# A graph layer: v projected inside the score stage and the skip term inside the aggregation, from stored parts

## The chip, the cores and the metric

The kernel runs on one core of a Trainium2 chip. The metric is the device time of one execution in microseconds (us), the median of several runs. Besides the runs there is one profiled execution, whose trace gives every time shown below. PE is the matmul engine, DVE, ACT and POOL are VectorE, ScalarE and GpSimd, SP is the engine that only issues transfers and waits. A q behind an engine's name (SPq, ACTq) marks what its sequencer does.

## What is computed

A graph layer on 2,500 nodes with 512 channels and 40,000 edges, then a global mixing block and a gated feed-forward block. The change touches only the graph layer's two attention rounds:

```
for l in range(2):
    q = (x @ Wq[l] + bq[l]).reshape(N, H, D)      # N 2500, H 8 heads, D 64
    k = (x @ Wk[l] + bk[l]).reshape(N, H, D)
    v = (x @ Wv[l] + bv[l]).reshape(N, H, D)
    a = (q[dst] * k[src]).sum(-1) / 8
    alpha = softmax of a over the edges with the same dst
    agg = segment_sum(alpha[:, :, None] * v[src], dst)
    x = agg + (x @ Ws[l] + bs[l]) + enc           # the skip term
```

The edges are sorted by dst. v is first needed when the scores are finished, the skip term only when the round is.

## The kernel before

The stages follow each other, with a barrier of all engines between them; per layer they are projection, score stage, softmax, aggregation.

**Projection** (`normalise_project` in the first layer, `combine_project` in the second). Rows are worked in 20 tiles of 128. PE transposes a tile (`flip`), ACT and DVE split it into a rounded part and a rest (`high`, `low`: `xT`), and for each of the four weights (s, k, v, q) PE runs 12 matmuls of 128x512 (three products of parts for each of four blocks of channels, `product`, L108). DVE adds bias (`add`); k and v go to HBM from ACT's queue, the skip sum `base` from SP's; q stays in SBUF as parts. The weights too are split before use (`w_highs` on ACT, `w_lows` on DVE, 16 blocks each). In the first layer the 33 blocks of the feed-forward weights are made ternary between the tiles: load (SP), `size`, `take`, `sign` (ACT), `choose` (DVE), transposes (PE), and for every third block a remainder (`low_unit` on DVE, `proj_rest`).

**Score stage** (`edge_attention`). POOL gathers the k rows of 128 edges with one indirect transfer of 256 KB (L1244, 313 of them, called edge tiles) into a ring of buffers, with four in flight (`FLIGHT = 4`: a gather waits until the fourth before it has landed). SP waits for each landing in order (`arrive`) and tells DVE. PE spreads the edges' destinations (L1445), ACT makes one-hot rows of them (L1392, L1398), PE picks the q rows with these (L1460), DVE multiplies them with the gathered k rows (L1296) and sums three quarters of the products, ACT the last quarter (L1385). The unit is a slot: an edge tile seen from one node tile. An edge tile that straddles two node tiles has two slots, so there are 332 slots (`USED`), in 83 batches of four; a slot's number runs ahead of its edge tile's number by the node tiles already finished, 0 to 19. The destinations come in rows of 8 slots, which SP loads in order between the `arrive`s. A ring buffer is free for gather t when `multiplied` has reached t - NB + NT + 1.

**Softmax** loads masks of 2 MB and lasts some 40 us. POOL meanwhile gathers the first v rows, up to 48.

**Aggregation.** DVE multiplies gathered v rows by their weights (L1373), PE sums them into the node tile with a one-hot matmul (L1506, four instructions a slot), ACT stores a finished node tile to HBM (`agg_rows`, 260 KB). DVE may be up to 16 slots ahead of PE (`R`).

Of the kernel before, what the change touches and what calls it, by code (L numbers as in the profile page):

```python
# [14 lines left out]
P = 128  # L15
N = 2500
C = 512
KC = C // P
# [25 lines left out]
NB = 40  # L44
# [88 lines left out]
def make_constants(nc, mem, T):  # L133

    T["ident"] = mem.sb("ident", [P, P])
    T["identb"] = mem.sb("identb", [P, P], BF16)
    T["lane"] = mem.sb("lane", [P, P])
    T["laneb"] = mem.sb("laneb", [P, P], BF16)
# [5 lines left out]
    ident, identb, lane, laneb = T["ident"], T["identb"], T["lane"], T["laneb"]  # L144
    with ExitStack() as stack:
# [3 lines left out]
        with nc.Block() as block:  # L149
# [14 lines left out]
            def _(vec):  # L164
                vec.wait_ge(built, 2)
                vec.tensor_copy(identb[:], ident[:]).then_inc(done, 1)
                vec.tensor_copy(laneb[:], lane[:]).then_inc(done, 1)
# [437 lines left out]
def normalise_project(nc, a, T, xn_dram, k_dram, v_dram, base_dram, ternary, names):  # L605

    with ExitStack() as stack:
# [3 lines left out]
        S_, K_, V_, Q_ = range(4)  # L612
# [7 lines left out]
        out = m.sb("out", [P, 2, 2, C])  # L620
        qsum = m.sb("qsum", [P, C])
        psT = [m.ps(f"psT{i}", [P, KC * P]) for i in range(2)]
        psP = [m.ps(f"psP{i}", [P, C]) for i in range(4)]
# [5 lines left out]
        kv_out = [m.sem(f"kv_out{b}") for b in range(2)]  # L629
# [28 lines left out]
        with nc.Block() as block:  # L658
            @block.sync
            def _(sp):  # L660
# [41 lines left out]
                for i in range(NT):  # L702
                    sp.wait_ge(ready, i * 4 + S_ + 1)
# [3 lines left out]
                    if i + XB < NT:  # L707

                        sp.wait_ge(turned, i + 1)
                        sp.wait_ge(biased, i + 1)  # L710
# [9 lines left out]
                sp.wait_ge(rest_out, 16 * FK)  # L720
                for b in range(2):
                    sp.wait_ge(base_out[b], 16 * (NT // 2))
# [4 lines left out]
            def _(pe):  # L727
# [19 lines left out]
                for i in range(NT):  # L747
# [3 lines left out]
                    for j in range(4):  # L751
                        if i:

                            pe.wait_ge(ready, i * 4 + j - 3)
                        else:
                            pe.wait_ge(w_lows, (j + 1) * KC)
# [10 lines left out]
            def _(act):  # L767
                def high(i):

                    act.wait_ge(turned, i + 1)  # L770
                    act.copy(xT[:, i % 2, 0].rearrange("p k n -> p (k n)"), psT[i % 2][:]).then_inc(xT_high, 1)
# [32 lines left out]
                for i in range(4 * KC):  # L804
                    act.copy(w[:, 0, i, :], T["w_rows"][:, i, :]).then_inc(w_highs, 1)
                    if i == KC - 1:
                        high(0)
                def q_part(i):
                    act.wait_ge(ready, i * 4 + Q_ + 1)
                    act.copy(qp[:, 0, i, :], qsum[:]).then_inc(rounded, 1)  # L810

                for i in range(NT):
                    if i + 1 < NT:
                        high(i + 1)
                    if i:
# [7 lines left out]
                    act.wait_ge(ready, i * 4 + K_ + 1)  # L823
                    act.dma_start(k_dram[i * P:(i + 1) * P, :], out[:, i % 2, K_ - 1, :]).then_inc(kv_out[i % 2], 16)
# [1719 lines left out]
```

## Time and profile before

| | |
|---|---|
| median of 3 runs | 3196.0 us (3192.7 to 3197.9) |
| profiled execution | 3192.6 us, of it 3190.5 us span of the trace |
| first layer: projection, score stage, softmax and aggregation | about 85 to 340, 341 to 763, to 1170 us |
| second layer: projection, then score stage to aggregation | about 1174 to 1425, to 2250 us |
| mixing, node MLP, feed-forward | to the end |
| PE busy, DVE, POOL, ACT | 79%, 68%, 52%, 36% of the span |

Busy shares are means over stages with different limits; a stage's limit is read from a stretch inside it.

### The profile page before, as it was taken

The numbers are of one execution on the slowest core, as the hardware profiler recorded it, in microseconds if no ns is written. First come the engines' busy times: TensorE is split into PE (matmuls) and PEld (weight loads), VectorE is DVE, ScalarE is ACT, GpSimd is POOL, SyncE is SP. The second block draws the span as 40 slices with busy tenths as digits, with TensorE's granted clock in tenths as the row PEclk, the third lists the DMA queues.
The fourth block names the chain that finished last, engine by engine and source line by source line (L and its number), as shares of the span: only waits on it lengthen the run. The fifth ranks groups of instructions, "written<-read, shape, count | busy, mean of one in ns | idle before, by whom it ended". The sixth has DMA issues, their size and how long they took to land. (4 is left out here: it accounts for less than half of the span.)

```text
span 3190.5 us, 46149 instructions
## 1 busy us (share of the span) xinstructions
PE 2531.2 (79%) x9872; PEld 1883.2 (59%) x9872; DVE 2171.0 (68%) x3512; ACT 1150.6 (36%) x4306; POOL 1644.5 (52%) x1559
## 2 busy tenths in 40 slices
PE   1999766664988879996666759888785999699998
PEld 1788444433776557874444448666564767477776
DVE  5766588888967765437888888777465454566665
ACT  0555466664000020016666610000353322155554
POOL 0101577777677741117777767777122443355555
PEclk9999787877999989997877769999887999899999
DMA  2565577776677774437777757777542332251111
GB/s 102 169 209 181 172 209 206 209 210 189 194 210 222 222 238 139 139 116 211 209 211 210 211 170 212 224 220 219 170 144 78 109 131 92 88 174 40 39 42 36
DMA packets 215857, 524.52 MB, mean 164 GB/s; under 512 B 30652, under 2 KB 48424, under 8 KB 215238
## 3 DMA queue, kind: packets, MB, share of 16 engines
q0 software_dynamic: 100160, 328.28, 35.5%
q1 hardware_dynamic: 98182, 161.91, 15.1%
q10 hardware_dynamic: 17280, 31.63, 2.6%
q8 instruction: 94, 1.54, 0.2%
q14 instruction: 141, 1.16, 0.1%
HBM read 439.83 MB, written 81.88 MB: 164 GB/s over the span
## 5 line engine op out<-in xcount | busy, mean ns | idle before, releaser
L1244 POOL DMA_INDIRECT edge_ring<-v_rows,edges_src x626 | 616.4, 985 | 237.3 <-issue 133.2
L1244 POOL DMA_INDIRECT edge_ring<-k_rows,edges_src x626 | 592.0, 946 | 252.9 <-issue 147.8
L1506 PE MATMUL edge_psA<-layer_q_space 128*128 128x256 f32 (+1 forms) x2656 | 639.0, 395 | 99.0 <-DVE layer_q_space L1373 90.8
L1506 PEld LDWEIGHTS edge_psA<-layer_q_space 128*128 128x128 f32 x2656 | 499.9, 194 | 237.8 <-issue 167.5
L1373 DVE TENSOR_TENSOR layer_q_space<-edge_ring,edge_psQ 128x512 f32<-128x512 f32 x664 | 431.9, 689 | 173.3 <-SPq L1213 136.8
L108 PE MATMUL proj_psP<-proj_w,proj_xT 128*128 128x512 f32 x1920 | 465.9, 400 | 7.0 <-DVE proj_xT L846 4.0
L1460 PE MATMUL edge_psQ<-layer_q_space,edge_hotT 128*128 x888 | 336.7, 527 | 132.8 <-ACT edge_hotT L1398 87.0
L1385 ACT ACTIVATE edge_ring<-edge_ring 128x64 f32<-128x64 f32 x1328 | 319.9, 242 | 286.2 <-DVE edge_ring L1296 286.2
L108 PEld LDWEIGHTS proj_psP<-proj_w,proj_xT 128*128 128x128 f32 x1920 | 359.7, 190 | 91.3 <-DVE proj_xT L846 4.4
L1296 DVE TENSOR_TENSOR edge_ring<-edge_psQ,edge_ring 128x512 f32<-128x512 f32 x444 | 286.4, 684 | 102.2 <-ACT edge_ring L1385 69.9
L1460 PEld LDWEIGHTS edge_psQ<-layer_q_space,edge_hotT 128*128 128x128 f32 x888 | 218.3, 257 | 218.6 <-issue 172.4
L1277 DVE TENSOR_REDUCE layer_scores<-edge_ring 128x24 f32<-128x1536 f32 x166 | 289.4, 1743 | 0.0
L2415 POOL TENSOR_TENSOR ffn_sums<-ffn_sums 128x512 f32<-128x512 f32 x110 | 173.0, 1573 | 199.2 <-DVE ffn_sums L2445 199.2
L1429 ACT COPY layer_q_space<-edge_psA 128x256 f32<-128x256 f32 x80 | 26.1, 379 | 688.2 <-PE edge_psA L1506 688.2
L1385 ACT ACTIVATION_READ_ACCUMULATOR edge_ring<-edge_ring 128x1 f32 x1328 | 247.6, 186 | 0.0
L1460 PE MATMUL edge_psA<-layer_q_space,edge_hotT 128*128 x440 | 169.2, 520 | 62.2 <-ACT edge_hotT L1398 39.1
L1296 DVE TENSOR_TENSOR edge_ring<-edge_psA,edge_ring 128x512 f32<-128x512 f32 x220 | 142.5, 684 | 49.1 <-ACT edge_ring L1385 37.4
L1460 PEld LDWEIGHTS edge_psA<-layer_q_space,edge_hotT 128*128 128x128 f32 x440 | 106.5, 254 | 105.2 <-issue 82.8
L2384 ACT ACTIVATE ffn_sums<-ffn_psP,kept_means 128x512 f32<-128x512 f32 x220 | 139.3, 684 | 79.7 <-PE ffn_psP L2339 78.5
L2445 DVE SCALAR_TENSOR_TENSOR ffn_sums<-ffn_psP,kept_means,ffn_sums 128x512 f32<-128x512 f32 x220 | 154.6, 743 | 17.1 <-PE ffn_psP L2339 16.6
L108 PE MATMUL ffn_psO<-ffn_downT,ffn_hT 128*128 128x512 f32 x660 | 153.2, 391 | 0.0
L1445 PE MATMUL edge_psA<-layer_y_space,edge_ones 1*128 1x512 bf16 x166 | 76.3, 462 | 90.1 <-DMA layer_y_space<-local_rows 90.0
(295 smaller groups left out, 3442.3 us busy)
## 6 DMA issues: line engine op xcount, KB each, us to landing
agg_rows<-layer_q_space ACTq DMA_DIRECT2D x40, 260.0 KB, 4.0
base_rows<-proj_enc SPq DMA_DIRECT2D x40, 256.0 KB, 2.1
k_rows<-proj_out ACTq DMA_DIRECT2D x40, 256.0 KB, 3.4
v_rows<-proj_out ACTq DMA_DIRECT2D x40, 256.0 KB, 2.5
edge_ring<-k_rows,edges_src POOLq DMA_INDIRECT x626, 3.7
edge_ring<-v_rows,edges_src POOLq DMA_INDIRECT x626, 3.7
ffn_downT<-down_rows SPq DMA_DIRECT2D x11, 512.0 KB, 10.2
proj_agg<-agg_rows SPq DMA_DIRECT2D x20, 260.0 KB, 3.1
```

Source lines behind the costliest of these rows:

```text
L108: last = pe.matmul(out, left[i], right[j], start=start and n == 0, stop=stop and n == 2)
L1244: pool.indirect_dma_start(ring[:, buffer[n], :], None, rows, bass.IndirectOffsetOnAxis(ap=T["src"][:, t:t + 1], axis=0)).then_inc(landed[b ...
L1277: vec.tensor_reduce(scores[:, j * B * H:(j * B + V) * H], prod[:, at:at + V, :].rearrange("p i (h d) -> p i h d", h=H), AX.X, ALU.add).the ...
L1296: vec.tensor_tensor(prod[:, s % (2 * B), :], psQ[s % QB][:], one(ring[:, bass.ds(arrived[i] % NB, 1), :]), ALU.mult).then_inc(multiplied, 1)
L1373: vec.tensor_tensor(wv[:, s % R, 0:C].rearrange("p (h d) -> p h d", h=H), ring[:, bass.ds(arrived[s % B] % NV, 1), :].rearrange("p o (h d) ...
L1385: act.activation(at, at, ACT.Copy, accum_out=scores[:, s * H + head:s * H + head + 1]).then_inc(reduced_act, 1)
L1445: pe.matmul(psB[j % 2], ones[:], rows_at[k % 2][0:1, at * P:at * P + B * P], start=True, stop=True).then_inc(spread, 1)
L1460: last = pe.matmul(psQ[(j * B + i) % QB][:], hotT[j % 2][:, i * P:(i + 1) * P], one(qp[:, k, bass.ds(tiles[i], 1), :]), start=(k == 1), st ...
L1506: last = pe.matmul(psA[:, bass.ds(d % 2, 1), e, 0:hi - lo].rearrange("p o w -> p (o w)"), hot[:, s % R, :], wv[:, s % R, lo:hi], start=Fal ...
L2384: act.activation(sums[:, f % 2, j, k, :], psP[k][:], ACT.Copy, scale=W["means"][:, j, f * KC + k:f * KC + k + 1]).then_inc(scaled, 1)
L2415: pool.tensor_tensor(sums[:, f % 2, j, 0, :], sums[:, f % 2, j, 0, :], sums[:, f % 2, j, 1, :], ALU.add).then_inc(summed, 1)
L2445: vec.scalar_tensor_tensor(out=half, in0=psP[k][:], scalar=W["means"][:, j, f * KC + k:f * KC + k + 1], in1=half, op0=ALU.mult, op1=ALU.ad ...
```

## The change

Both projections now compute k and q only. They store to HBM the split tile (`later_v["xT"]`, 512 KB a tile) and, at the fifth tile, the split weights of v and s (2 MB each) and the bias of v in two parts; `base` is now x plus the bias and skips the product. In the score stage SP loads the v weights once, and the split tiles in halves of 256 KB (`load_half`, three buffers); PE projects one tile of v over three batches (`project_v`), ACT copies the result (`keep_v`) and stores it to HBM. In the aggregation the same is done for the skip term (`project_skip`, one of four blocks of channels a batch); SP loads the stored `base` tile, DVE adds the product (`add_skip`), SP stores it again. The room comes from the ring: k has 28 buffers in place of 40; PE's result buffers for picked q rows go from six to five. The gathers of v wait until all v tiles are stored.

```diff
-NB = 40
+NB = 28
...
-                    for j in range(4):
+                    for j in range(2):
...
                 for i in range(NT):
-                    sp.wait_ge(ready, i * 4 + S_ + 1)
+                    sp.wait_ge(xT_ready, i + 1)
+                    sp.dma_start(later_v["xT"][i * P:(i + 1) * P, :], xT[:, i % 2].rearrange("p h k n -> p (h k n)").bitcast(F32)
+                                 ).then_inc(xT_out[i % 2], 16)
+                    if i == KC:
+                        sp.wait_ge(w_lows, 4 * KC)
+                        for name, j in (("w", V_), ("skip_w", S_)):
+                            sp.dma_start(later_v[name].rearrange("p (h k c) -> p h k c", h=2, k=KC),
+                                         w[:, :, j * KC:(j + 1) * KC, :].bitcast(F32)).then_inc(v_parts_out, 16)
...
-                for i in range(4 * KC):
+                for i in range(2 * KC):
+                    w_low(i)
...
+                    if i < KC:
+                        w_low(2 * KC + 2 * i)
+                        w_low(2 * KC + 2 * i + 1)
...
-                    add(i, S_)
                     add(i, K_)
...
-                    add(i, V_)
                     for u in units(i):
                         choose(u)
+                    add(i, Q_)
                     for u in units(i - 1):
                         low_unit(u)
-                    add(i, Q_)
...
+        V_AT = [3 + i * 10 // 3 for i in range(NT)]
+            for n, k in ((0, 0), (1, 1), (2, 2), (2, 3)):
+                v_steps.setdefault(at + n, []).append((i, k))
...
+        S_AT = [2 + 4 * i for i in range(NT)]
+        s_steps = {S_AT[i] + k: (i, k) for i in range(NT) for k in range(KC)}
...
+                for h in range(XH, 2 * NT):
+                    halves_by_block.setdefault((batch_of(h - XH) + 5) // 2, []).append(h)
...
+                for h in range(XH, 2 * NT):
+                    i, half = divmod(h - XH, 2)
+                    beside_block.setdefault((S_AT[i] + 1 + 2 * half) * B + 3 * B, []).append((load_half, 2 * NT + h))
+                for i in range(NT):
+                    beside_block.setdefault((S_AT[i] + 9) * B, []).append((store_base, i))
+                    if i + 2 < NT:
+                        beside_block.setdefault((S_AT[i] + 11) * B, []).append((load_base, i + 2))
                 sp.sem_inc(v_arrived, V_FIRST - 1)
                 for t in range(ET):
                     arrive(ET + t, v_arrived)
+                    for do, i in beside_block.pop(t, ()):
+                        do(i)
...
+                pool.wait_ge(v_stored, 16 * NT)
                 for t in range(ET):
...
+                        if V_AT[i] + 3 == j:
+                            keep_v(i)
...
+                    for i, k in v_steps.get(j, ()):
+                        project_v(i, k)
                     pe.wait_ge(hotT_ready, j + 1)
...
                 for s in range(USED):
+                    if s % B == 0 and s // B in s_steps:
+                        project_skip(*s_steps[s // B])
```

`beside_block` is keyed by the edge tile at whose arrival SP issues the transfer; `S_AT` and `V_AT` count batches of four slots. Three places show how the order moves.

SP in the first projection, one tile of rows, before (`base_rows` is the skip sum's store, `proj0_raw` and the ..._rows of `proj0_mag` and `proj0_rest` are the feed-forward blocks):

```order
L704 DMA base_rows<-proj0_enc 128x512
L670 DMA xn_rows<-proj0_x 128x512
L663 DMA proj0_x<-x 128x512
L694 DMA down_rows<-proj0_mag 128x512
L697 DMA down_rows<-proj0_rest 128x512
L691 DMA gate_rows<-proj0_mag 128x512
L684 DMA proj0_raw<-L0_ffn_w_gate 128x512
L684 DMA proj0_raw<-L0_ffn_w_up 128x512
```

and the fifth tile now:

```order
L703 DMA v_xT<-proj0_xT 128x1024
L708 DMA v_w<-proj0_w 256x1x2048
L708 DMA v_skip_w<-proj0_w 256x1x2048
L711 DMA v_bias<-proj0_bias_parts 1x1024
L714 DMA base_rows<-proj0_enc 128x512
L669 DMA xn_rows<-proj0_x 128x512
L662 DMA proj0_x<-x 128x512
L690 DMA up_rows<-proj0_mag 128x512
L693 DMA down_rows<-proj0_mag 128x512
L696 DMA down_rows<-proj0_rest 128x512
L683 DMA proj0_raw<-L0_ffn_w_down 128x4x128
L683 DMA proj0_raw<-L0_ffn_w_gate 128x512
```

The split tile's store stands ahead of everything in each tile, and here the two weight stores of 2 MB stand ahead of the row loads and the loads of feed-forward blocks.

SP from the first score stage to the next projection, before:

```order
L1209 UNCONDITIONAL_BRANCH
L1222 DMA layer0_y_space<-local_rows 1x1024 x41
L1222 DMA layer0_y_space<-local_rows 1x512
L1230 DMA layer0_q_space<-mask_rows 128x8066
L1208 UNCONDITIONAL_BRANCH
L978 UNCONDITIONAL_BRANCH
L981 DMA proj1_agg<-agg_rows 128x520
```

Nothing stands there in the aggregation. Now, the start of the score stage (`v_w` are the v weights, `x_halves<-v_xT` the halves):

```order
L1316 DMA edge0_ring<-local_rows 1x1024
L1320 DMA edge0_ring<-v_w 128x4096
L1322 DMA edge0_ring<-v_bias 2x512
L1296 DMA edge0_x_halves<-v_xT 128x2x256 x3
L1316 DMA edge0_ring<-local_rows 1x1024 x4
L1296 DMA edge0_x_halves<-v_xT 128x2x256
L1316 DMA edge0_ring<-local_rows 1x1024
L1296 DMA edge0_x_halves<-v_xT 128x2x256
L1316 DMA edge0_ring<-local_rows 1x1024
```

and the end of the aggregation with the next projection's first load:

```order
L1296 DMA edge0_x_halves<-v_xT 128x2x256
L1348 DMA base_rows<-layer0_q_space 128x512
L1296 DMA edge0_x_halves<-v_xT 128x2x256
L1344 DMA layer0_q_space<-base_rows 128x512
L1296 DMA edge0_x_halves<-v_xT 128x2x256
L1348 DMA base_rows<-layer0_q_space 128x512
L1344 DMA layer0_q_space<-base_rows 128x512
L1348 DMA base_rows<-layer0_q_space 128x512 x2
L1281 UNCONDITIONAL_BRANCH
L1002 UNCONDITIONAL_BRANCH
L1005 DMA proj1_agg<-agg_rows 128x520
```

The last half, the last load of `base` and the last three stores are issued from the last edge tiles' arrivals on.

PE in the score stage, the start of a batch before (L1445 spreads the next batch, L1460 picks q rows):

```order
L1445 MATMUL edge0_psA<-layer0_y_space,edge0_ones 128x512
L1131 TENSOR_LOAD edges_numbers
L1131 ISA x8
L1460 ISA
L1460 MATMUL edge0_psQ2<-layer0_q_space,edge0_hotT 128x512
```

and now (L1613 and L1653 are these two; `ones_r` brings in the bias, `x_halves` are the v matmuls):

```order
L1613 MATMUL edge0_psA<-edge0_ring,edge0_ones 128x512
L1181 TENSOR_LOAD edges_numbers
L1181 ISA x8
L1631 MATMUL edge0_psA<-edge0_ring,edge0_ones_r 128x512
L108 MATMUL edge0_psA<-edge0_ring,edge0_x_halves 128x512 x3
L1653 ISA
L1653 MATMUL edge0_psA<-layer0_q_space,edge0_hotT 128x512
L1653 ISA
L1653 MATMUL edge0_psA<-layer0_q_space,edge0_hotT 128x512
```

The v matmuls, with their waits for a half and for the last copy, stand between the spread and the picked rows of the batch.

## Rows read from the trace of the kernel before

**Rows 1.** Stretches of five stages: length, busy us (instructions) of each engine, clock, DMA, GB/s.

```profile
120.00:310.00 190.00, 190.00 (x913) 155.38 (x911) 127.42 (x343) 102.96 (x383) 21.26 (x17) 1.00 0.60 202
1210.00:1390.00 180.00, 180.00 (x807) 145.59 (x806) 89.21 (x158) 17.67 (x32) 21.09 (x16) 1.00 0.42 141
450.00:720.00 270.00, 175.86 (x488) 108.11 (x487) 224.72 (x272) 173.84 (x973) 201.69 (x214) 0.80 0.72 208
840.00:880.00 40.00, 40.00 (x184) 34.72 (x183) 37.09 (x75) 1.26 (x3) 29.85 (x33) 1.00 0.74 215
880.00:1150.00 270.00, 228.67 (x928) 173.36 (x927) 190.80 (x364) 20.10 (x48) 196.92 (x209) 0.97 0.74 219
```

**Rows 2.** Timeline of PE, first layer's projection: start, length, instructions.

```profile
200.90 0.60 PE L732 MATMUL proj_psT<-kept_ident,proj_x 128*128 128x128 f32 x4
201.26 5.85 PE L108 MATMUL proj_psP<-proj_w,proj_xT 128*128 128x512 f32 x24
...
213.42 0.60 PE L732 MATMUL proj_psT<-kept_ident,proj_x 128*128 128x128 f32 x4
```

**Rows 3.** Timeline of all engines, first layer's projection.

```profile
213.53 0.69 DVE L877 TENSOR_TENSOR proj_rest<-proj_psW,proj_mag 128x512 fp32r<-128x512 f32 x1
...
215.09 0.45 SPq L684 DMA_DIRECT2D proj_raw<-L_ffn_w_gate  x1
...
218.21 0.31 ACT L781 ACTIVATE proj_mag<-proj_raw 128x128 f32<-128x128 f32 x1 [1.53 <-DMA proj_raw<-L_ffn_w_gate]
...
220.57 1.04 ACT L800 CAST proj_mag<-proj_psW 128x512 fp32r<-128x512 f32 x2
...
221.52 1.15 ACT L786 ACTIVATE proj_raw<-proj_raw 128x512 f32<-128x512 f32 x2
```

**Rows 4.** Waits in the score stage: us in total, times, longest.

```profile
POOL edge_ring L1244 <- issue: 58.2, 191, 0.3
...
PE edge_psA L1445 <- DMA layer_y_space<-local_rows: 40.3, 20, 3.2
...
POOL edge_ring L1244 <- DMA edge_ring<-k_rows,edges_src: 4.4, 5, 1.3
```

**Rows 5.** Line L1244, first 61 us of the score stage: count, ns min/median/max, first and last start.

```profile
L1244 POOL DMA_INDIRECT edge_ring<-k_rows,edges_src x49: 942/946/1123, 340.9 to 401.1; - x49
```

**Rows 6.** Line L1296 in the same stretch.

```profile
L1296 DVE TENSOR_TENSOR edge_ring<-edge_psQ,edge_ring x28: 680/682/692, 348.8 to 397.4; 128x512 f32<-128x512 f32 x28
L1296 DVE TENSOR_TENSOR edge_ring<-edge_psA,edge_ring x14: 680/682/693, 353.8 to 399.5; 128x512 f32<-128x512 f32 x14
```

**Rows 7.** Gathers (tile edge_ring on POOL) in the score stage, 450 to 720.

```profile
DMA to landing us min/median/max: 3.3/3.7/5.7
```

**Rows 8.** The same in the aggregation, 880 to 1150.

```profile
DMA to landing us min/median/max: 3.2/3.7/6.5
```

**Rows 9.** Waits in the aggregation, 880 to 1150.

```profile
POOL edge_ring L1244 <- DMA edge_ring<-v_rows,edges_src: 13.9, 17, 2.1
```

**Rows 10.** DMA issues in the same stretch: count, KB each, median us to landing.

```profile
agg_rows<-layer_q_space ACTq DMA_DIRECT2D x16, 260.0 KB, 4.0
```

**Rows 11.** Timeline where the masks are loaded, after the scores.

```profile
757.36 0.35 SPq L1230 DMA_DIRECT2D layer_q_space<-mask_rows  x1
...
763.40 0.94 POOL L1244 DMA_INDIRECT edge_ring<-v_rows,edges_src  x1 [2.28 <-DMA edge_ring<-v_rows,edges_src]
...
767.61 0.94 POOL L1244 DMA_INDIRECT edge_ring<-v_rows,edges_src  x1 [3.27 <-DMA edge_ring<-v_rows,edges_src]
```

**Rows 12.** DMA of the second projection, 1210 to 1390.

```profile
q1 hardware_dynamic: 9216, 16.85, 29.9%
...
proj_x<-base_rows SPq DMA_DIRECT2D x16, 256.0 KB, 3.6
```

**Rows 13.** Timeline of the aggregation's end.

```profile
1162.01 7.31 PE L1506 MATMUL edge_psA<-layer_q_space 128*128 128x256 f32 x32 [0.92 <-DVE layer_q_space L1373]
...
1166.06 1.29 DVE L1373 TENSOR_TENSOR layer_q_space<-edge_ring,edge_psQ 128x512 f32<-128x512 f32 x2 [0.64 <-SPq L1213]
```

More of the change, by code:

```diff
@@ L611, in normalise_project @@
         RAW = 4
-        S_, K_, V_, Q_ = range(4)
+        K_, Q_, S_, V_ = range(4)
         raw = m.sb("raw", [P, RAW, C])
@@ L881, in _, with w_low @@
                 normalise(1)
-                for i in range(4 * KC):
+                def w_low(i):
                     vec.wait_ge(w_highs, i + 1)
@@ L1089, in _, with w_low @@
                 combine_tile(1)
-                for i in range(4 * KC):
+                def w_low(i):
                     vec.wait_ge(w_highs, i + 1)
@@ L1186, in edge_attention @@
         pse, psb = psQ[2][0:H, 0:2 * CH], psQ[2][:, 2 * CH:4 * CH]
+        psS = [psQ[i][:] for i in range(2)]
         wt = psQ[3][:, 0:16 * H].rearrange("p (s u h) -> p s u h", s=2, h=H)
@@ L1234, in _ @@
                     arrive(ET + t, v_arrived)
+                    for do, i in beside_block.pop(t, ()):
+                        do(i)
+                for t in sorted(beside_block):
+                    for do, i in beside_block[t]:
+                        do(i)
+                for b in range(2):
+                    sp.wait_ge(base_out[b], 16 * (NT // 2))
             @block.gpsimd
@@ L1376, in _ @@
                                       ALU.mult).then_inc(weighted, 1)
+                for i in range(NT):
+                    if (S_AT[i] + 7) * B + 1 >= USED:
+                        add_skip(i)
             @block.scalar
@@ L1446, in spread_row, with spare_row, project_v @@
                               ).then_inc(spread, 1)
+                bases = nc.alloc_registers(f"v_parts_at{layer}", engines=[pe.engine])
+                nc.regs_mov(bases, NB)
+                base = nc.snap(bases, min_val=NB, max_val=NB + 1)
+                def spare_row(n, rows=slice(0, P)):
+                    return one(ring[rows, bass.ds(base + n, 1), :].bitcast(F32R))
+                def project_v(i, k):
+                    if k == 0:
+                        if i == 0:
+                            pe.wait_ge(wv_in, 32)
+                            pe.wait_ge(ones_high, 1)
+                        else:
+                            pe.wait_ge(v_kept, i)
+                        pe.matmul(psV, ones_r[:], spare_row(2 * KC, slice(0, 2)), start=True, stop=False)
+                    h = 2 * i + k // 2
+                    if k % 2 == 0:
+                        pe.wait_ge(half_in[h % XH], h // XH * 16 + 16)
+                    product(pe, psV, [x_halves[:, h % XH, part, k % 2, :] for part in range(2)],
+                            [spare_row(part * KC + k) for part in range(2)], start=False, stop=(k == KC - 1)
+                            ).then_inc(v_projected, 1)
                 pe.wait_ge(built, 1)
```

258 lines of the change are left out of this document (195 added, 63 removed).

## The prediction

> **What bounds the kernel now.** I read the table of stretches first [rows 1]. In both projections PE is busy without a gap at full clock, so a projection is as long as its matmuls. The first layer's timeline gives the unit: from one tile's transposes to the next it is 213.42 - 200.90 = 12.5 us, of which 24 products (two weights) take 5.85 [rows 2]. The second layer runs 807 PE instructions in 180 us, 52 a tile, so 11.6 us a tile.
>
> In the score stage and the aggregation PE is not the limit (65% and 85% busy [rows 1]). There POOL's chain of gathers is. It waits 191 times 0.3 us, the price of issuing, and almost never longer [rows 4]; with 0.95 us for the gather itself [rows 5] that is 1.25 us per edge tile, 313 of them. The score stage follows POOL although DVE and ACT look idle: SP loads the destination rows of the next eight slots only between arrivals, so PE waits 2 us for such a row in 20 blocks of a stretch of 320 us [rows 4]. Any delay of a gather therefore lengthens the stage.
>
> How much delay a gather bears follows from FLIGHT = 4. Four starts are 5.0 us apart, less 0.3: a gather may take 4.7 us to land. The median is 3.7 in both stages [rows 7, 8], so 1.0 us is spare. The one other traffic of the aggregation is the store of a finished node tile, 260 KB [rows 10]. Next to these 16 stores POOL waits 17 times for a landing, 13.9 us in all, with the slowest landing at 6.5 [rows 8, 9]. Less 0.3 each that is 8.8 us, **0.55 us of POOL's chain per store**; in the score stage, without such traffic, the same row has 4.4 us in 5 waits [rows 4].
>
> **What the change gives, first layer.** The removed products are 5.85 us of 12.5 a tile. I do not count all of it, since another loop closes behind PE in the 17 tiles with feed-forward blocks. A remainder ends on DVE at 213.53 + 0.69 = 214.2; SP stores it and only then, at 215.09, issues the next load; ACT waits for that load until 218.21, sizes, copies until 221.6 and signs until 222.7 [rows 3]. That is 8.5 us. Then follow comparisons of the second block (1.1), the addition of q (0.7) and the next remainder (0.7): 11.0 us, 11.5 with a store of 512 KB more in the queue. Two of three tiles carry a remainder; for the third I take 9.5 to 10, so a mean of 11.0. The 17 tiles gain 1.5 each, 25 us, the other three 5.6 each, 17. Eight weight splits before the first tile fall away (5 us) and come back in tiles 0 to 3 (5 us). The 4 MB of weight stores at the fifth tile stand ahead of row loads; at 0.62 us per 256 KB (below) they take 10 us, of which one tile's lead hides half: 5 us lost. Sum **-37 us**, bounds -20 (loop slower still) and -112 (PE alone, 20 x 5.6).
>
> **Second layer.** No such loop. PE would need 11.6 - 5.6 = 6.0 us a tile; DVE is busy 89.2 us in 15.5 tiles [rows 1], 5.8 less two additions, 4.4. SP's loop waits for its own `base` store behind 512 KB of xT, then loads. Transfers were 42% busy at 141 GB/s [rows 1]; 1.8 MB a tile at the same efficiency are 5.4 us. With three things near 6 I take 6.7: 20 x 4.9 = 98, less 5 for the weight splits in the first tiles and 6 for the 4 MB bubble (tiles are shorter, the lead too). Sum **-87 us**, bounds -60 and -112.
>
> **What it costs, per layer.** All prices are on POOL's chain.
>
> *Start of the score stage.* SP issues the 2 MB of v weights and three halves, 2.75 MB, beside the first gathers. The nearest rows are the mask load of 2 MB: issued at 757.36, POOL then waits 2.28 and 3.27 us [rows 11], 5.0 above the usual, or 0.62 us per 256 KB. Eleven such pieces give 6.8; I take 6. Bounds 0 and 8.
>
> *Score stage.* 37 halves and 20 stores of v. A store as measured, 0.5. A load has no isolated row: from the mask, 0.62 would stay inside the spare 1.0 and cost nothing; read as sustained it costs 0.62. The own time of transfers in the second projection speaks for the upper half (29.9% of 180 us for 64 on SP's queue is 0.84 us each [rows 12]). I take 0.3. Six blocks load two halves at once, 0.5 more each. 20 x 0.5 + 37 x 0.3 + 3 = 24; bounds 10 and 40.
>
> *The smaller ring* lets gather t start when t - 7 slots are multiplied. In the first 61 us POOL starts 49 gathers and DVE 42 products [rows 5, 6], six ahead of the finished ones: the limit is not touched, by one slot. Late landings will touch it: 3 us, bounds 0 and 10. The v matmuls themselves, 13 a tile, lie in PE's idle third, the copies on ACT (0.7 us in three batches) in its waits.
>
> *Softmax.* 2.75 MB of skip weights and halves behind the masks; the first v rows have some 7 us of slack: 2 us.
>
> *Aggregation.* 37 halves, 18 loads and 20 stores of `base`: 20 x 0.5 + 55 x 0.3 = 27, bounds 10 and 45. PE needs 40 / 184 x 4 = 0.87 us a slot [rows 1] and 0.16 more for the skip products, still under the 1.25 of an edge tile; 20 additions on DVE lie in its idle 30%.
>
> *End of the aggregation.* The halves are issued by edge tile, but needed by slot. The half for batch S_AT[i] is issued at tile 4 S_AT[i] - 8, while slots run ahead of tiles by up to 19. So late in the stage PE waits for halves and falls behind. The last half is issued at the arrival of tile 312, the very last, and is needed in batch 80, slot 320. Such a load lands in 3.6 us [rows 12], say 4 with the wait; then 12 slots remain, 12 x 0.87 plus 6 products, 11.8. The stage would end 15.8 us after the last arrival; now it is 1169.3 - 1166.1 = 3.3 [rows 13]. **+12.5 us**, bounds 8 and 17. The `base` stores end within it.
>
> A layer costs 6 + 24 + 3 + 2 + 27 + 12.5 = 74.5, both 149.
>
> **The sum.** 3192.6 (the profiled execution) - 37 - 87 + 149 = 3217.6. It lies 3.4 us under the median of the runs, so I predict **3220 us**, 0.8% over the median. A difference under 0.2% (6.4 us) is about what a measurement of this kernel cannot tell from none.
>
> **The rivals.** *The transfers are hidden* (other side). It happens if a transfer of 256 KB lengthens a gather by less than the spare 1.0 us; then POOL never waits for it, and 24 and 27 fall to 10 (the stores) or 0. For it: the mask's 0.62 per 256 KB, and that the new transfers in the aggregation stand four edge tiles, 5 us, apart. Against it: the 0.55 of each store, also alone. With 0 to 20 a layer for the two and the rest as above the time is 3192.6 - 124 + 47 + (0 to 40), 3116 to 3156, say 3135 with the 3.4. It decides at 0.75 of the prices I take: the sum is zero when transfers cost 39 a layer in place of 51.
>
 The landing of 6.5 beside a store [rows 8] is 2.8 over the median, more than such sharing explains, so the trace goes against it for stores and leaves it open for loads.
>
> *The projections fall to PE's floor*: both gain 112, 3192.6 - 224 + 149 = 3118. For it: DVE 67% and transfers 60% busy in the first [rows 1]; against it the remainder's loop, which already makes ACT wait 1.53 us for a load [rows 3].
>
> *PE's own waits bound the score stage* (same side as the forecast). Twelve of the 37 halves are needed in the very batch that starts when they are issued, and the copy of a tile by ACT stands before the next tile's first product. If each holds the picked rows by 2 us and DVE cannot make it up in its waits, 12 x 2 + 13 x 1 = 35 a layer come on top: 3290. Against it: PE idles a third, and a block has some 2 us of waiting for rows.
>
> **Chances.** The forecast 0.50 (3200 to 3250), hidden transfers 0.25, the floor 0.08, PE's waits 0.17. Faster takes the second and third and a little of the first: 0.35; same 0.08; slower 0.57. For eight in ten the range takes the forecast, most of PE's waits and the upper two thirds of hidden transfers: 3125 to 3290; for the forecast alone it is 3180 to 3260, from the bounds of its largest terms.
>
> **What would show it.** Right: first-layer tiles of about 11 us with PE idle behind DVE and ACT, second-layer tiles of 6.7; POOL's waits for landings in the score stage up from a few us to 25, in the aggregation to 35 a layer; PE waiting for `x_halves` in the last third of the aggregation, and its last slots some 16 us after the last arrival. Wrong: POOL's waits stay under 10 us (hidden), or first-layer tiles of 7 to 8 us, or long waits of POOL for the ring behind DVE's products, which I price at 3 us.

## The result, and the profile after

The change makes the kernel slightly faster: 3178.1 us median of five runs (3170.1 to 3180.0) against 3192.9 of the kernel before, beside it on the same chip; the ratio is 0.9944, 95% interval 0.9930 to 0.9958. The forecast was 3220, so the time lies inside its range and on the other side of no change. The profiled execution took 3170.1 us, 3168.4 of it span. It is the fastest of the five, 8 us under their median, which has to be kept in mind where its stages are added up.

The stages, from the two traces (a score stage from the first gather of k to the last product, an aggregation from the first weighted row to PE's last product, the second projection between an aggregation's end and the next gather of k):

| us | before | after | change | forecast |
|---|---|---|---|---|
| start and first projection | 340.9 | 315.4 | -25.5 | -37 |
| score stages | 419.9, 415.5 | 439.6, 440.0 | +19.7, +24.5 | +33 each |
| softmax | 43.8, 45.3 | 45.6, 43.9 | +1.8, -1.4 | +2 each |
| aggregations | 364.7, 365.3 | 390.2, 390.4 | +25.5, +25.1 | +39.5 each |
| - of it POOL's chain of v gathers, first to last start | 425.5, 425.7 | 438.0, 436.7 | +12.5, +11.0 | +27 |
| - of it from the last gather's start to PE's end | 7.4, 7.9 | 22.1, 20.9 | +14.7, +13.0 | +12.5 |
| second projection | 255.8 | 165.6 | -90.2 | -87 |
| the rest | 939.3 | 937.7 | -1.6 | 0 |

The sum is -22.1, which is 3190.5 to 3168.4. (The chain begins in the softmax, so its two lines don't add up to an aggregation exactly.) The projections gave 116 us and the attention stages took 95 back, where 149 was forecast.

Stretches of the changed kernel in the columns of [rows 1]:

```profile
120.00:285.00 165.00, 118.00 (x489) 91.77 (x488) 101.34 (x276) 87.73 (x336) 19.10 (x14) 0.84 0.67 241
450.00:720.00 270.00, 211.78 (x647) 136.38 (x646) 217.31 (x262) 175.32 (x952) 194.32 (x206) 0.82 0.79 240
880.00:1150.00 270.00, 247.72 (x1066) 202.89 (x1065) 197.48 (x379) 18.03 (x43) 192.53 (x205) 0.98 0.84 265
1205.00:1345.00 140.00, 122.06 (x520) 96.57 (x521) 99.79 (x163) 29.33 (x53) 29.42 (x20) 0.92 0.86 303
```

PE no longer fills the first projection: 72% busy at a granted clock of 0.84, where it was full at 1.00. In the score stage and the aggregation the DMA engines are at 0.79 and 0.84 of their time in place of 0.72 and 0.74, and POOL starts 206 and 205 gathers in 270 us.

POOL's waits in us, times and longest: for landings in the score stage (450 to 720), then in the aggregation (880 to 1150) for landings and for ring buffers behind DVE's products, to be laid beside [rows 4] and [rows 9]. The last line is the kernel before, for the ring, in the same aggregation stretch; for landings it has 3.3 us in 4 waits in the score stretch.

```profile
POOL edge_ring L1379 <- DMA edge_ring<-k_rows,edges_src: 15.2, 23, 1.8
...
POOL edge_ring L1379 <- DMA edge_ring<-v_rows,edges_src: 23.4, 39, 1.2
...
POOL edge_ring L1379 <- DVE layer_q_space L1521: 19.3, 51, 1.8
...
POOL edge_ring L1244 <- DVE layer_q_space L1373: 13.2, 40, 1.1
```

and the time from a gather's start to its landing in the same two stretches, beside [rows 7] and [rows 8]:

```profile
DMA to landing us min/median/max: 3.3/3.9/6.2
...
DMA to landing us min/median/max: 3.5/4.4/5.7
```

In the aggregation the median gather lands 0.7 us later than before, still under the 4.7 that four in flight allow. POOL waits more often, 39 times in place of 17, but each wait is shorter: less 0.3 each they sum to 11.7 us where before had 8.8. By the same reckoning the waits for the ring come to 4.0 us in place of 1.2. The two differences, 5.7 us, are about the four gathers fewer (205 in place of 209, 5 us) that start in this stretch.

The first projection's timeline, one turn of the loop through the remainder, and PE's transposes of a tile of rows, which give the pitch:

```profile
212.66 0.60 PE L743 MATMUL proj_psT<-kept_ident,proj_x 128*128 128x128 f32 x4
...
225.87 0.60 PE L743 MATMUL proj_psT<-kept_ident,proj_x 128*128 128x128 f32 x4
...
239.39 0.60 PE L743 MATMUL proj_psT<-kept_ident,proj_x 128*128 128x128 f32 x4
...
244.35 0.68 DVE L896 TENSOR_TENSOR proj_rest<-proj_psW,proj_mag 128x512 fp32r<-128x512 f32 x1
...
245.05 0.32 SPq L696 DMA_DIRECT2D down_rows<-proj_rest  x1
...
245.89 0.45 SPq L683 DMA_DIRECT2D proj_raw<-L_ffn_w_gate  x1
...
248.26 0.60 PE L743 MATMUL proj_psT<-kept_ident,proj_x 128*128 128x128 f32 x4
...
249.84 0.31 ACT L794 ACTIVATE proj_mag<-proj_raw 128x128 f32<-128x128 f32 x1 [2.95 <-DMA proj_raw<-L_ffn_w_gate]
...
253.15 1.15 ACT L799 ACTIVATE proj_raw<-proj_raw 128x512 f32<-128x512 f32 x2
...
253.88 2.19 DVE L884 SCALAR_TENSOR_TENSOR proj_raw<-proj_mag,proj_half,proj_raw 128x128 f32<-128x128 f32 x8
...
255.99 0.68 DVE L928 TENSOR_TENSOR proj_qsum<-proj_psP,proj_bias 128x512 f32<-128x512 f32 x1
256.59 0.68 DVE L896 TENSOR_TENSOR proj_rest<-proj_psW,proj_mag 128x512 fp32r<-128x512 f32 x1
...
256.73 5.09 PE L108 MATMUL proj_psP<-proj_w,proj_xT 128*128 128x512 f32 x12 [4.66 <-DVE proj_qsum L928]
```

The loop is the one of the forecast: remainder, its store, the next load, ACT's wait of 2.95 us for it, sizes, signs, comparisons, q's addition, the next remainder: 256.59 - 244.35 = 12.2 us. PE waits 4.66 us for DVE at its end. Three tiles take 13.2, 13.5 and 8.9 us.

The end of the first aggregation:

```profile
1168.67 0.94 POOL L1379 DMA_INDIRECT edge_ring<-v_rows,edges_src  x1 [0.43 <-DMA edge_ring<-v_rows,edges_src]
...
1173.66 0.53 SPq L1296 DMA_DIRECT2D edge_x_halves<-v_xT  x1
...
1178.50 1.06 PE L108 MATMUL edge_psQ<-layer_q_space,edge_x_halves 128*128 x3
...
1183.61 7.18 PE L1722 MATMUL edge_psA<-layer_q_space 128*128 128x256 f32 x32
```

SP issues the last half when the last gather has landed (1173.66), and PE ends 17.1 us later.

### The profile page after: what moved, and what is told of

Same layout as the page of the kernel before. It is cut to its first block and busy times, and to the rows that moved or that the text cites. A ratio compares the mean times of both kernels' runs of the same rounds, so it can differ in the third digit from the quotient of the medians.

```text
span 3168.4 us, 46710 instructions
## 1 busy us (share of the span) xinstructions
PE 2538.9 (80%) x9912; PEld 1903.6 (60%) x9912; DVE 2153.6 (68%) x3472; ACT 1169.6 (37%) x4350; POOL 1645.7 (52%) x1559
## 5 line engine op out<-in xcount | busy, mean ns | idle before, releaser
L1722 PEld LDWEIGHTS edge_psA<-layer_q_space 128*128 128x128 f32 x2656 | 514.4, 195 | 138.6 <-issue 53.8
L1435 DVE TENSOR_TENSOR edge_ring<-edge_psQ,edge_ring 128x512 f32<-128x512 f32 x532 | 346.5, 683 | 143.4 <-ACT edge_ring L1536 71.2
L1653 PE MATMUL edge_psQ<-layer_q_space,edge_hotT 128*128 x1064 | 362.8, 476 | 59.8 <-ACT edge_hotT L1561 34.9
L1653 PEld LDWEIGHTS edge_psQ<-layer_q_space,edge_hotT 128*128 128x128 f32 x1064 | 240.7, 233 | 151.0 <-issue 96.3
L108 PE MATMUL proj_psP<-proj_w,proj_xT 128*128 128x512 f32 x960 | 267.6, 437 | 64.7 <-DVE proj_qsum L928 50.2
L108 PEld LDWEIGHTS proj_psP<-proj_w,proj_xT 128*128 128x128 f32 x960 | 197.9, 211 | 122.2 <-DVE proj_qsum L928 57.7
L108 PE MATMUL edge_psA<-edge_ring,edge_x_halves 128*128 x480 | 167.2, 477 | 37.4 <-DMA edge_x_halves<-v_xT 18.7
L108 PE MATMUL edge_psQ<-layer_q_space,edge_x_halves 128*128 x480 | 167.3, 456 | 22.3 <-DMA edge_x_halves<-v_xT 22.2
L108 PEld LDWEIGHTS edge_psA<-edge_ring,edge_x_halves 128*128 128x128 f32 x480 | 93.5, 217 | 85.5 <-issue 49.5
L108 PEld LDWEIGHTS ffn_psO<-ffn_downT,ffn_hT 128*128 128x128 f32 x660 | 123.0, 188 | 25.2
```

Of the source, the lines that this page charges most:

```text
L108: last = pe.matmul(out, left[i], right[j], start=start and n == 0, stop=stop and n == 2)
L1435: vec.tensor_tensor(prod[:, s % (2 * B), :], psQ[s % QB][:], one(ring[:, bass.ds(arrived[i] % NB, 1), :]), ALU.mult).then_inc(multiplied, 1)
L1653: last = pe.matmul(psQ[(j * B + i) % QB][:], hotT[j % 2][:, i * P:(i + 1) * P], one(qp[:, k, bass.ds(tiles[i], 1), :]), start=(k == 1), st ...
L1722: last = pe.matmul(psA[:, bass.ds(d % 2, 1), e, 0:hi - lo].rearrange("p o w -> p (o w)"), hot[:, s % R, :], wv[:, s % R, lo:hi], start=Fal ...
```

## The experiments

Each ran with the kernel before on the same chip; ratios are to that kernel, with 95% intervals. It took 3193.4 us beside the kernels of the next three headings, and 3187.3 to 3187.7 beside the others (the kernel without loads and stores among them), so ratios compare and times don't quite. The changed kernel's ratio is 0.9944. Stages are read from one trace of each kernel. Where no edit touched them, chains of gathers differ by up to 6 us between traces (436.7 and 442.8 for the changed kernel's second chain of v, the longer one from the kernel with the remainder's store moved), and the part behind the graph layer takes 937.0 to 946.0; a few us in a single stage show little.

**Transfers of the aggregation by slot.**

```diff
+                by_slot, beside_block = beside_block, {}
+                for s in sorted(by_slot):
+                    beside_block.setdefault(s * ET // USED, []).extend(by_slot[s])
                 for t in range(ET):
                     arrive(ET + t, v_arrived)
```

> The changed kernel, with one edit: in the aggregation SP issues the halves and the loads and stores of base at the edge tile that belongs to their slot (key times 313/332) in place of an edge tile with the slot's number. Theory (late halves): the tail after the last gather's start, 22.1 and 20.9 us in the changed kernel against 7.4 and 7.9 before, shrinks to about 9, PE's waits for x_halves in the aggregation vanish, and the time falls by some 25 us to about 3153. Rival (PE is behind by its own work, four products for the slots and one for the skip term, whatever SP does): the tail stays above 18 us and the time within 8 us of 3178.

3155.9 us, ratio 0.9880 (0.9857 to 0.9904). The tail fell to 7.9 us in both layers, the value of before, so the late issue was its cause, and PE's own work was not; PE's waits for `x_halves` from 1000 to 1170 (11.4 us in the changed kernel) are gone. The chains of v gathers grew from 438.0 and 436.7 to 445.5 and 443.6, which takes back half of the tail. Only three transfers in each layer, a half, a load and a store of `base`, moved from behind the last gather's start to before it; at the prices found below they don't explain 7 us, and the cause stays open. POOL's waits for landings in 880 to 1150:

```profile
POOL edge_ring L1382 <- DMA edge_ring<-v_rows,edges_src: 27.8, 36, 1.9
```

**Without the loads, without the stores, without either.** The three edits leave the semaphore's count and drop the transfer, as here for the halves:

```diff
+                    if h % (2 * NT) >= XH:
+                        sp.sem_inc(half_in[h % XH], 16)
+                        return
                     sp.dma_start(x_halves[:, h % XH].bitcast(F32).rearrange("p h k n -> p h (k n)"),
```

> The changed kernel without the transfers of the halves but the first three of each stage, and without the loads of base but the first two of each layer; all waits and matmuls stay, on stale data, so the output lacks them. Theory A (the forecast's prices, 0.3 us of POOL's chain per load): score stage 14 us shorter, aggregation 16 to 20 shorter, in each layer, time about 3110 to 3118. Theory B (loads are hidden inside a gather's spare time, and stores and the smaller ring make the lengthening): score stage and chain of v gathers change by less than 4 us each, only the tail loses a landing of some 4 us per layer, time 3160 to 3175.

> The changed kernel without the stores of base in both aggregations and without the stores of v in the second score stage; the adds and copies stay, so the output lacks the skip term and the second layer's v. Theory A (0.5 us of POOL's chain per store, as before's agg_rows): each aggregation's chain of gathers 10 us shorter, the second score stage 10 shorter, the first unchanged, time about 3148. Theory B (stores are hidden too, and something else lengthens the stages): each stage within 3 us, time 3170 to 3178.

> The changed kernel without the repeated loads (halves, base), without the stores of base, and without the second layer's stores of v; matmuls, copies and additions stay (stale data, so the output lacks skip term and v). Theory A (the lengthening of the chains is transfers alone, and loads and stores overlap in what they cost): the chain of v gathers returns to 424 to 427, as before the change, though without loads alone it was 432 and without stores alone 435 to 441; the second score stage comes to 420 to 425. Theory B (PE's and DVE's added work lengthens them): chains above 430.

Without loads the time is 3137.2 us, ratio 0.9832 (0.9806 to 0.9858); without stores 3167.3, 0.9914 (0.9894 to 0.9934); without either 3119.9 in a single execution. The stages, in us:

| | score chains | v chains | tails |
|---|---|---|---|
| before | 394.3, 391.2 | 425.5, 425.7 | 7.4, 7.9 |
| after | 414.0, 415.5 | 438.0, 436.7 | 22.1, 20.9 |
| without loads | 405.8, 405.1 | 432.1, 431.4 | 17.6, 17.4 |
| without stores | 416.9, 410.7 | 440.8, 434.8 | 21.1, 21.2 |
| without either | 406.2, 399.8 | 426.1, 427.4 | 17.3, 17.2 |

Neither price held. Without the loads the score chains are 8 and 10 us shorter, where the forecast's prices give 14, and the v chains 6 and 5, where they give 16.5. The stores of `base`, taken away while loads remain, change the v chains by +3 and -2, where 10 was forecast; v's own stores, which are dropped in the second score stage alone, are worth 4.7 us there, 0.24 each. With both away the v chains are back at before's within a few us, in this single execution, so the transfers are the lengthening there (theory A of the third run). Whether the prices add is open in the aggregation: 5 to 6 us for the loads, nothing clear for the stores and 9 to 12 for both are as far apart as unedited chains. In the second score stage the single traces do add up, 10.4 and 4.7 against 15.7 for both. Of the 8.6 that remain there over before, 3.9 are the start of the stage (the first 27 gathers take 37.7 us in place of 33.8) and 3.1 are longer waits for the ring; 1.6 stay open.

**The smaller ring alone.** The kernel before with `NB = 28`.

> The kernel before, with a ring of 28 buffers for k in place of 40 (and the products' buffers at its end, as in the changed kernel). The forecast's price: 3 us a layer at most and only with late landings, so 0 to 4 us in all, 3193 to 3197. Rival (the ring itself holds POOL, as its waits for DVE's products went from 20 to 35 and 30 us): 7 us a layer, about 3207.

3195.1 us, ratio 1.0005 (0.9995 to 1.0015): no difference. The score chains are 395.3 and 392.8, 1.0 and 1.6 longer. By itself the smaller ring costs no more than the 3 us a layer of the forecast, and the longer waits for the ring in the changed kernel (35 and 30 us in place of 20) are not the ring's own: here they are 25 and 22.

**The remainder's store behind the loads.** In the first projection SP's order is changed:

```diff
                     for u in units(i + 1):
                         if i:
                             load_unit(u)
+                    for u in units(i - 1):
+                        store_rest(u)
```

> The changed kernel, with one edit in the first projection: SP stores the remainder of a feed-forward block behind the next tile's two loads of blocks in place of ahead of them. Theory (the forecast's loop through the remainder's store bounds the tiles): the tiles with a remainder, 13.3 us apart in the changed kernel, fall to 9 to 10, the first projection ends 30 to 45 us earlier and the time is about 3140. Rival (the blocks' loads wait for something else, or the lower granted clock of PE holds the tiles): less than 8 us, 3170 to 3178.

3155.3 us, ratio 0.9900 (0.9884 to 0.9917). The first gather of k starts at 287.4 in place of 315.4, 28 us earlier, a little under the 30 to 45 of the theory. In the timeline the loads now stand ahead of the remainder, and three tiles take 12.0, 8.9 and 9.2 us:

```profile
210.37 0.60 PE L750 MATMUL proj_psT<-kept_ident,proj_x 128*128 128x128 f32 x4
...
222.41 0.60 PE L750 MATMUL proj_psT<-kept_ident,proj_x 128*128 128x128 f32 x4
...
223.64 0.70 SPq L683 DMA_DIRECT2D proj_raw<-L_ffn_w_gate  x1
...
227.37 0.68 DVE L903 TENSOR_TENSOR proj_rest<-proj_psW,proj_mag 128x512 fp32r<-128x512 f32 x1
...
228.08 0.33 SPq L701 DMA_DIRECT2D down_rows<-proj_rest  x1
...
231.29 0.60 PE L750 MATMUL proj_psT<-kept_ident,proj_x 128*128 128x128 f32 x4
...
240.48 0.60 PE L750 MATMUL proj_psT<-kept_ident,proj_x 128*128 128x128 f32 x4
```

By the ratios only 14 us of the 28 arrive. In the profiled execution the second chain of v gathers took 442.8 us against 436.7 in the changed kernel, and the tails 23.9 and 24.7, although nothing was edited there: its aggregations are 9 us longer in all. No run shows why.

**Six gathers in flight.**

```diff
-                FLIGHT = 4
+                FLIGHT = 6
```

> The changed kernel with six gathers in flight in place of four, so that a gather may take 7.2 us to land in place of 4.7. Theory A (what the transfers cost is late landings, which POOL then waits for): its waits for landings, 14 to 28 us a stage above the usual price of issuing, fall to under 4, the score stage by some 12 and the chain of v gathers by some 20 in each layer, time about 3120. Theory B (the DMA engines themselves are short of time, so that waiting is only put off): the waits turn into waits for the ring or for arrivals, stages within 5 us, time 3165 to 3185.

> The kernel before with six gathers in flight in place of four. Theory A (a gather is made late only by the transfers beside it; before has such transfers in the aggregation alone): the chains of v gathers fall by some 10 us to 415, the score stages stay within 3 us, time about 3170. Then the change is worth some 70 us with six in flight against 15 with four. Theory B (six in flight is simply faster for gathers, with or without other transfers): the score stages fall too, and before gains as much as the changed kernel did, some 75 us, to about 3115.

The changed kernel: 3100.4 us, ratio 0.9726 (0.9705 to 0.9748). Before: 3170.8, ratio 0.9959 (0.9943 to 0.9975). In the aggregation of the changed kernel with six in flight, 880 to 1080, POOL's waits, the gathers and their landing are:

```profile
POOL edge_ring L1379 <- issue: 32.6, 107, 0.3
POOL edge_ring L1379 <- DVE layer_q_space L1521: 16.1, 53, 0.3
```

```profile
L1379 POOL DMA_INDIRECT edge_ring<-v_rows,edges_src x160: 942/946/962, 880.2 to 1078.9; - x160
...
DMA to landing us min/median/max: 3.5/4.6/6.4
```

and in the changed kernel itself:

```profile
L1379 POOL DMA_INDIRECT edge_ring<-v_rows,edges_src x152: 940/946/955, 879.6 to 1080.0; - x152
```

With six in flight 160 gathers start in (1078.9 - 880.2) us, 1.250 each, in place of 1.327, and no row names a landing. They land no sooner (4.6 in the middle, 6.4 at most), but nobody waits for it. The v chains are 415.1 and 417.6, the score chains 395.9 and 401.3. The kernel before gains in its aggregations (v chains 413.5 and 416.0 against 425.5 and 425.7) and hardly in its score stages (390.2 and 390.1 against 394.3 and 391.2, and 391.3 with four in flight in the kernel of the next heading), as theory A has it: its stores of finished node tiles make gathers late in the aggregation, and it has nothing of the kind in the score stage. The quotient of the two ratios is 0.977: with six in flight the change is worth 2.3%, with four 0.6%.

**The price of before's store.** The second layer's stores of finished node tiles left out, and in another kernel cut to 512 of 520 columns.

> The kernel before without the second layer's stores of finished node tiles (the output lacks that layer's sums; the first layer is unchanged and the comparison is inside the run). The forecast's price (0.55 us of POOL's chain per store): the second layer's chain of v gathers is 10 us shorter than the first's, 415 against 425.5, and POOL's waits for landings fall from 21 to a few us. Rival (these waits stand beside the stores by chance, or the chain is set elsewhere): the same chain within 3 us.

> The kernel before, where the second layer stores only 512 of the 520 columns of a finished node tile (rows of 2,048 bytes as base and v have, in place of 2,080; the output lacks the denominators). If the price of 0.55 us belongs to the odd row, the second layer's chain falls by most of 10 us as without stores; if it belongs to any store, the chain stays within 2 us of 425.5.

Without them the second chain is 417.1 us and the first, with its stores, 425.8: 8.8 us for 20 stores, 0.44 each, in one execution. The waits below, less the usual 0.3 each, fall from 7.7 to 2.3 us, 0.34 for each of the stretch's 16 stores. So the 0.55 that the forecast read from [rows 8, 9] put some waits on the stores that come without them too; it was high by a quarter or more for that store. With 512 columns the chain is 426.2, also in one execution: the odd row is not the reason. POOL's waits without the stores, second layer (1960 to 2230), then with them, first layer (880 to 1150) of the same kernel:

```profile
POOL edge_ring L1244 <- DMA edge_ring<-v_rows,edges_src: 4.1, 6, 1.0
...
POOL edge_ring L1244 <- DMA edge_ring<-v_rows,edges_src: 12.5, 16, 1.6
```

**The edits together, and the weight stores in pieces.** The second kernel has the three edits, and replaces the two stores of 2 MB at the fifth tile by one piece of 256 KB in each tile from there on.

```diff
+                    if i >= KC:
+                        name, j = (("w", V_), ("skip_w", S_))[(i - KC) // (2 * KC)]
+                        half, k = divmod((i - KC) % (2 * KC), KC)
+                        sp.dma_start(later_v[name].rearrange("p (h k c) -> p h k c", h=2, k=KC)[:, half, k, :],
+                                     w[:, half, j * KC + k, :].bitcast(F32)).then_inc(v_parts_out, 16)
```

> The changed kernel with the three edits together: transfers of the aggregation by slot, the remainder's store behind the loads, six gathers in flight. If the three act on separate waits, 3178 less 78, 20 and up to 25: about 3055 to 3065. Rival (with gathers in time PE sets the aggregation, slots and skip products, so that the earlier halves give nothing): 3080 or more.

> The same three edits, and the 4 MB of v and skip weights are stored in 16 pieces of 256 KB, one a tile behind the tile's loads, from the fifth tile on, in both projections. Theory (the forecast's 5 and 6 us of standstill at the fifth tile): both bubbles go, 8 to 12 us less than with the three edits alone. Rival (the pieces cost as much, spread over the tiles, since the second projection's transfers were 90% busy beside them): within 4 us of it, or slower.

The three together: 3045.9 us, ratio 0.9564 (0.9546 to 0.9582), where their sum would be 0.9618; the tails are 9.1 and 8.6 us, so the earlier halves pay, and the chains (414.9 and 416.4) don't lengthen for it once gathers are waited for in time. With the pieces: 3034.1, ratio 0.9529 (0.9510 to 0.9547), 12 us less. This is 4.7% under the kernel before and 4.2% under the changed one. In the trace the projections gain 10.5 and 10.9 us, more than the theory's 8 to 12 for both, and 6 us of it are lost again behind the graph layer, which was not edited; that the time fell by 12 is in part luck. In the second projection about 7 us come from the two tiles behind the weight stores and the rest from later tiles, which are 6.0 us long in place of 6.4 to 6.6. That projection now runs at PE's own speed with the DMA engines at 0.96 of their time. Its stretch 1170 to 1245, and, of the changed kernel, the standstill behind the weight stores:

```profile
1170.00:1245.00 75.00, 75.00 (x350) 61.35 (x349) 53.67 (x102) 13.26 (x24) 16.11 (x12) 1.00 0.96 331
```

```profile
1252.00:1280.00 28.00, 23.33 (x97) 18.38 (x96) 16.12 (x28) 4.43 (x8) 5.42 (x4) 0.88 0.93 329
```

## Why the prediction was wrong, step by step

**The step that failed** is the price of the transfers, the terms "20 x 0.5 + 37 x 0.3 + 3 = 24" and "20 x 0.5 + 55 x 0.3 = 27". Each layer was to lose 51 us of POOL's chain to them. What dropping them gave back is 15.7 us in the second layer's score stage and 9.3 to 11.9 in the aggregations, 25 to 28 a layer. The forecast had written that its sign turns at 39, and it did. In the aggregation the mechanism was right: POOL waits for late landings beside transfers, and with six in flight these waits are gone in the stretch shown and the v chains come within 1.6 us of those of the kernel before with six. The size was wrong. A load was priced at 0.3 and measured 0.22 to 0.28 in the score stages (8.2 and 10.4 us for 37) and 0.10 in the aggregations (5.9 and 5.3 for 55); v's store was priced at 0.5 and measured 0.24; all 75 transfers of an aggregation together cost 0.12 to 0.16 each, where a store of a finished node tile, among gathers with no other transfers, cost 0.44. Over the first layer's whole chain of v gathers, before and after, POOL's waits for landings are:

```profile
POOL edge_ring L1244 <- DMA edge_ring<-v_rows,edges_src: 21.2, 23, 3.3
...
POOL edge_ring L1379 <- DMA edge_ring<-v_rows,edges_src: 41.1, 54, 4.1
```

So 75 more transfers brought 31 more waits (32 in the second layer): most of them leave the gathers (4.4 us to landing in the middle) inside the 1.0 us that is spare. Whether some also share a late gather, so that POOL waits once for two of them, is a guess that no run tests. Nor does any run tell whether the queue matters: the stores that gave 0.44 are issued by ACT, halves and `base` by SP.

In the score stage another wait grew, which the forecast priced at 3 and named as a sign of being wrong: POOL's for the ring behind DVE's products. In 340 to 735, before, after, and after with six in flight:

```profile
POOL edge_ring L1244 <- DVE edge_ring L1296: 20.7, 64, 0.8
...
POOL edge_ring L1379 <- DVE edge_ring L1435: 35.7, 89, 1.3
...
POOL edge_ring L1379 <- DVE edge_ring L1435: 32.8, 93, 1.1
```

Less 0.3 each these are 1.5, 9.0 and 4.9 us, and 0.8, 8.7 and 10.1 in the second layer: over a third of what the first layer's score stage lost, and, with the start of the stage, nearly all that it still loses with six in flight. The smaller ring alone makes 3.3 and 1.6, and without loads and stores the second layer's are 3.9: a half of them hangs on the transfers, as a guess by way of late landings. What PE's products of v, ACT's copies and the smaller ring each add to the rest was not taken apart.

**Hidden transfers**, the rival with the other sign, was thus half right: 3135 was its time, 3178 came. The rule that it rested on in the Trainium skill (DMA: Bandwidth & Descriptors, section Queues, rings and completion order), that engines take turns between queues packet by packet, agrees with the 0.7 us by which the median landing grew: the own time of a transfer on SP's queue was 0.84 in [rows 12]. What the rule alone doesn't give is the tail of landings over 4.7 us, which makes most of the aggregation's cost here.

**The first projection** gave 25.5 of 37. Loop and order were as predicted; the mean pitch of the three tiles shown is 11.9 us in place of 11.0 (the load lands 3.95 us after its issue, 3.1 in [rows 3], and the second comparison ends later). Taking the remainder's store out of the loop showed the loop to be the bound, 28 us. The weight stores cost a little more than the 5 us predicted: the two tiles behind them are 18.7 and 14.6 us long in place of 13.3 each, 6.7 in all, and with the loop gone their pieces gave 10.5.

**The second projection** was right: 6.0 to 6.6 us a tile where 6.7 was said, and a standstill of 6.6 us over two tiles where 6 was said; -90 against -87. That the later tiles were held at 6.4 to 6.6 by the weight stores showed only when these came in pieces.

**The end of the aggregation** was right: PE ends 17.1 us behind the last arrival (15.8 predicted), and the tail grew by 14.7 and 13.0 (12.5 predicted). PE's waits for `x_halves` late in the stage are there, 11.4 us in 9 waits from 1000 to 1170 and none from 880 to 1000. Issuing by slot removed the tail, but with four in flight the chains of gathers grew by half of it.

**The smaller terms**: start of the score stage 4 to 5 for 6 predicted, the ring alone 1 to 1.6 for 3, with the waits of the changed kernel 7.5 and 7.9, softmax 0 for 2. PE's waits as that rival had them, 35 a layer more (its own sum, 12 x 2 + 13 x 1, is 37), did not come: with six in flight and all v matmuls in place the chains are 5.7 and 11.2 us over those of the kernel before with six. A part of this size may still be theirs, in the waits for the ring.

By stages the miss of 47 us in the profiled execution is 22 in the score stages, 28 in the aggregations and 8 elsewhere on one side, and 11.5 in the first projection on the other.

## What to carry to other kernels

A price per transfer, read where transfers are rare, must not be multiplied by a large count: ask first how much lateness the consumer bears, and whether added transfers can fall on the same gather. Where a chain waits at a fixed number of transfers in flight, try a larger number before and after such a change; here it decides whether moving work beside the gathers is worth 0.6% or 2.3%. Work that is issued by one counter and needed by another drifts apart towards the end of the stage, and big one-off stores are better placed in pieces between the regular ones, which gave 21 us in the two projections' traces.

## What was not expected of the hardware

With six in flight gathers start 1.25 us apart in the aggregation with the DMA engines at 0.87 of their time (880 to 1080), so the engines were not short; with the weight stores in pieces the second projection even ran undisturbed at 0.96 and 331 GB/s.

Behind a wait PE's products were slower: 12 of them take 5.09 us behind an idle stretch of 4.66, where [rows 2] has 24 in 5.85. The granted clock of that stage is 0.84, a mean between its two levels, where before, without gaps, it was 1.00. In that tile this cost nothing: the transposes behind the slow products end at 262.7, and ACT, which needs them, measures block sizes until 263.9. In the tile without a remainder ACT did wait for them:

```profile
269.75 5.39 PE L108 MATMUL proj_psP<-proj_w,proj_xT 128*128 128x512 f32 x12 [3.82 <-DVE proj_qsum L928]
...
275.61 0.59 ACT L813 CAST proj_mag<-proj_psW 128x512 fp32r<-128x512 f32 x1 [1.71 <-PE proj_psW L754]
```

Up to 1.7 us in a third of the tiles may thus belong to the clock; no run separates it from the loop.

Why 20 stores of `base` cost 4 to 6 us without the loads (without loads against without either) and nothing measurable beside them stays open; unedited chains differ as much. So does why the profiled execution lies 8 us under its median: the part behind the graph layer took 937.7 us in it, near the low end of 937.0 to 946.0, and its chains of gathers could be some us shorter than in the other executions, which no trace shows.
